# Spherical numbers of three chunks copied over rows by DMA, and both edge-weight layers in fp32 on two row halves

## What is computed

```python
wk = relu(edge_features @ k_w1 + k_b1) @ k_w2 + k_b2      # 64 -> 64 -> 128, and the same for wv
k  = wk * sum_s sh[e, s] * (x_dst @ Cqk[:, s, :])          # s = 0..8: nine spherical numbers of an edge
v  = wv * sum_s sh[e, s] * (x_dst @ Cv[:, s, :])
attn = sum over each head of q[edge_src] * k               # then a softmax over the edges of a node
upd  = sum over the edges of a node of v * alpha
```

## Time and profile before

| | |
|---|---|
| Median of 3 runs | 2944.04 us (2942.39 to 2945.2) |
| Profiled execution, its time | 2947.53 us |
| Its span in the trace | 2945.7 us |
| Busy share of the span: PE, DVE, ACT, POOL | 84%, 89%, 51%, 59% |
| Granted TensorE clock, mean | 0.899 of full speed; 1.00 within the loop |
| Stages: before the loop / loop / behind it | about 0 to 485 / 485 to 2771 / to 2946 us |
| DMA in all | 415 MB, 141 GB/s mean |

### The profile page before, as it was taken

One profiled execution on the slowest core, in us unless ns is written; L12 is line 12 of the kernel. 1 busy time (PEld: TensorE's weight loads), 2 busy tenths in 40 slices (PEclk: granted clock), 3 DMA queues, 4 the chain that ended last, 5 costly groups with the idle time before them and its releaser, 6 DMA issues.

```text
span 2945.7 us, 48186 instructions
## 1 busy us (share of the span) xinstructions
PE 2469.1 (84%) x12310; PEld 1787.3 (61%) x12505; DVE 2612.7 (89%) x3389; ACT 1514.6 (51%) x2914; POOL 1731.3 (59%) x1719
## 2 busy tenths in 40 slices
PE   2233347999999999999999999999999999999714
PEld 1233315677777776777677776777677777777511
DVE  6688835899999999999999999999999999999737
ACT  1321224566666655666566665666566566666310
POOL 1800037777777766667676666666666677665030
PEclk7555557999999999999999999999999999999855
DMA  6787714245555544444444444444445544544340
GB/s 187 202 222 187 210 25 111 76 131 149 148 149 145 148 147 139 141 142 148 139 144 142 146 147 140 140 144 147 142 141 147 148 141 142 148 144 132 121 124 11
DMA packets 282407, 415.35 MB, mean 141 GB/s; under 512 B 64463, under 2 KB 191875, under 8 KB 278470
## 3 DMA queue, kind: packets, MB, share of 16 engines
q1 hardware_dynamic: 222278, 296.67, 32.4%
q0 software_dynamic: 52704, 107.19, 15.1%
q10 hardware_dynamic: 7128, 8.13, 0.8%
...
## 4 chain that ended last, share of the span: by engine, by line
PE 52%; DVE 7%; issue 6%; ACT 3%; DMA 2%; POOL 2%; SPq 0%; DVEq 0%; ACTq 0%; POOLq 0%
PE bank L1118 11%; PE bank L1120 9%; PE bank L1119 9%; PE bank L1142 5%; PE bank L1163 4%; PE bank L1194 2%; PE bank L1124 2%; PE bank L1125 2%; PE bank L1095 2%; PE bank L1113 2%; DVE xa_t L1538 1%; DVE z_l L1546 1%; PE bank L1102 1%; POOL gathered L745 1%; PE bank L1101 1%
## 5 line engine op out<-in xcount | busy, mean ns | idle before, releaser
L745 POOL DMA_INDIRECT gathered<-xtab_d,src_g x784 | 780.6, 996 | 449.7 <-PE bank L1095 203.0
L745 POOL DMA_INDIRECT gathered<-qtab_d,dst_g x784 | 801.9, 1023 | 257.2 <-issue 249.0
L1118 PE MATMUL bank<-z_h,wt_h 128*128 128x512 f32 x1568 | 729.6, 465 | 27.9 <-DVE val L1578 27.9
L1538 DVE TENSOR_TENSOR xa_t<-bank,r_r 128x512 f32<-128x512 f32 x980 | 667.3, 683 | 13.5 <-PE bank L1142 10.3
L876 ACT ACTIVATE z_h<-xa_t 128x512 fp32r<-128x512 f32 x980 | 617.4, 634 | 110.1 <-DVE xa_t L1538 100.3
L1120 PE MATMUL bank<-z_h,wt_l 128*128 128x512 f32 x1568 | 620.7, 396 | 0.0
L1119 PE MATMUL bank<-z_l,wt_h 128*128 128x512 f32 x1568 | 618.8, 395 | 0.0
L1546 DVE TENSOR_TENSOR z_l<-xa_t,z_h 128x1024 fp32r<-128x1024 f32 x392 | 478.0, 1219 | 48.2 <-ACT z_h L876 44.6
L1118 PEld LDWEIGHTS bank<-z_h,wt_h 128*128 128x128 f32 x1568 | 301.1, 192 | 131.4 <-issue 92.7
L869 ACT ACTIVATE hid<-bank,b1kv 128x512 f32<-128x512 f32 x196 | 134.8, 688 | 476.4 <-PE bank L1102 462.4
L1120 PEld LDWEIGHTS bank<-z_h,wt_l 128*128 128x128 f32 x1568 | 294.9, 188 | 69.2
...
## 6 DMA issues: line engine op xcount, KB each, us to landing
nrow_d<-x_r SPq DMA_DIRECT2D x196, 288.0 KB
ea<-in_ea_t SPq DMA_DIRECT2D x392, 128.0 KB
exb<-exd_d SPq DMA_DIRECT2D x392, 128.0 KB
dmb<-exd_d SPq DMA_DIRECT2D x392, 128.0 KB
ea_c<-in_ea_t SPq DMA_DIRECT2D x49, 512.0 KB, 5.0
aggrow_d<-xa_t SPq DMA_DIRECT2D x49, 512.0 KB, 3.9
gathered<-xtab_d,src_g POOLq DMA_INDIRECT x784
gathered<-qtab_d,dst_g POOLq DMA_INDIRECT x784
```

The source lines that it names most:

```text
L745: rows_in = pool.indirect_dma_start(rows[:, c % 4, k, :], None, table, bass.IndirectOffsetOnAxis(ap=picked[:, s, at:at + 1], axis=0))
L1118: pe.matmul(ps[:, :], wt_h[rows, w, :], high, start=start, stop=False)
L1538: dve.tensor_tensor(z[:, i, :], bank[2 + (NJ * c + i) % 2][:, :], xt[:, c % 2, :], ALU.mult).then_inc(z_ok, 1)
```

## The change

- Chunks 0 and 1 (`NS = 2`) are spread by the TensorE as before, each now with a bank of its own. For chunks 2 to 4, SP's new `load_harmonics` issues six DMAs for each group, two groups ahead: each reads one row of 512 fp32 numbers from DRAM and writes it to 64 partitions of `sh_b` (two buffers).
- `outer` for chunks 2 to 4 is one multiplication of 128 x 1536 elements with both inputs in SBUF, in place of three of 128 x 512 with one input in PSUM. `outer_high` for them is one copy of 1536 elements in place of three.
- Both weight layers are done in fp32, without splits. `ea2` holds edges 0 to 255 on partitions 0 to 63 and edges 256 to 511 on 64 to 127, and the two loads of it are half as large. `hidden` is two fp32 matmuls of 256 columns, one on each row half, into banks 2 and 3 (the spread banks, free by then); it moves from before the products to behind `weights` and is done a body earlier. `weights` is four fp32 matmuls of 256 columns, for k on rows 0 to 63 and for v on rows 64 to 127 in turn.
- `edge_high`, `edge_low`, `hidden_low` and one of the two steps of `front_h` go; `front_h` is two steps of 256 columns in place of two of 512. The orders of the lists of ACT and DVE change as shown; `key_query` comes behind `sum_values`.
- Waits go with this: the spreads of group c wait for `hid_ok` of that group (ACT has read the banks), `hidden` waits for the two multiplications that read them, `load_edge` waits for `hid_ps` in place of `eal_ok`.
- The weights of the two layers leave the split table (`NW` 12 to 10), `exb` moves into a free part of `x_r`, and addresses in the loads are formed by round and place within it (`columns`).

The diff, cut to its core:

```diff
-CK, CV, W2KV, W1KV = 0, NJ, 2 * NJ, 2 * NJ + 1
-NW = 2 * NJ + 2
+CK, CV, CEND = 0, NJ, 2 * NJ
+NW = CEND
+NS = 2
+NZ = 3
...
-        ea2 = sb("ea2", [P, 2, G])
-        ea_hl = sb("ea_hl", [P, 2, G], F32R)
-        exb = sb("exb", [P, 2, G])
+        ea2 = sb("ea2", [P, 2, HG])
+        sh_b = sb("sh_b", [P, 2, NJ - NS, G])
...
             def load_edge(j, c):
-                past(sp, eal_ok, j, c, 2)
+                past(sp, hid_ps, j, c, 2, 2)
                 hold()
                 for half in range(2):
-                    sp.dma_start(ea2[half * D:(half + 1) * D, c % 2, :], edges_t[:, bass.ds(group(j, c) * G, G)]
-                                 ).then_inc(ea_in[c % 2], 16)
-                past(sp, shb_ps, j, c, 4, NJ)
+                    sp.dma_start(ea2[half * D:(half + 1) * D, c % 2, :],
+                                 columns(edges_t, j, c)[:, half * HG:(half + 1) * HG]).then_inc(ea_in[c % 2], 16)
+                past(sp, shb_ps, j, c, 4, NS)
                 hold()
                 if not isinstance(j, int) or c >= 2:
                     landed(sp, s3_in, j, c - 2)
                 hold()
-                sp.dma_start(s3[0:SP3, c % 4, :], sh3_d.rearrange("a s e -> (a s) e")[:, bass.ds(group(j, c) * G, G)]
-                             ).then_inc(s3_in[c % 2], 16)
+                sp.dma_start(s3[0:SP3, c % 4, :], columns(sh3_d.rearrange("a s e -> (a s) e"), j, c)).then_inc(s3_in[c % 2], 16)
+
+            def load_harmonics(j, c):
+                past(sp, z_ok, j, c, 2, NZ)
+                hold()
+                for i in range(NS, NJ):
+                    for half in range(2):
+                        k = min(2 * i + half, S - 1)
+                        sp.dma_start(sh_b[half * D:(half + 1) * D, c % 2, i - NS, :],
+                                     columns(harmonics_t[k:k + 1, :], j, c).to_broadcast([D, G])
+                                     ).then_inc(sh_b_in[c % 2], 16)
...
             def body(j, c):
+                if live(j, c + 2):
+                    load_harmonics(j, c + 2)
                 if live(j, c + 3):
...
-            def edge_high(j, c):
-                landed(act, ea_in, j, c, 32)
-                past(act, hid_ps, j, c, 2)
-                act.activation(ea_hl[:, c % 2, :], ea2[:, c % 2, :], ACT.Copy).then_inc(eah_ok, 1)
             def front_h(j, c):
-                done(act, hid_ps, j, c)
+                done(act, hid_ps, j, c, 2)
+                past(act, wk_ps, j, c, 1)
                 past(act, wv_ps, j, c, 1)
-                act.activation(hid[:, :], ps_hw[:, :], ACT.Relu, bias=b1kv[:, :]).then_inc(hid_ok, 1)
-                act.activation(hid_h[:, :], ps_hw[:, :], ACT.Relu, bias=b1kv[:, :]).then_inc(hid_ok, 1)
+                for f in range(2):
+                    act.activation(hid[:, f * HG:(f + 1) * HG], bank[2 + f][:, 0:HG], ACT.Relu, bias=b1kv[:, :]
+                                   ).then_inc(hid_ok, 1)
 
             def outer_high(j, c, i):
                 if i == 0:
                     past(act, acc_ps, j, c, 2)
-                done(act, z_ok, j, c, NJ, i + 1 - NJ)
-                act.activation(z_h[:, c % 2, i, :], z[:, i, :], ACT.Copy).then_inc(zh_ok, 1)
+                done(act, z_ok, j, c, NZ, i + 1 - NZ)
+                chunks = slice(i, i + 1) if i < NS else slice(NS, NJ)
+                act.activation(z_h[:, c % 2, chunks, :], z[:, chunks, :], ACT.Copy).then_inc(zh_ok, 1)
 
             def front_q(j, c):
                 done(act, qt_ps, j, c)
...
@@ -918,8 +939,6 @@
                                .rearrange("p f h w -> p (f h) w"), ACT.Copy).then_inc(row_ok, 1)
 
             def body(j, c):
-                if live(j, c + 1):
-                    front_h(j, c + 1)
                 s = batch_at(c, 8)
                 if live_batch(j, s):
                     batch_scores(j, s)
@@ -937,13 +956,11 @@
                 if live_batch(j, s):
                     batch_turned(j, s)
                 if live(j, c + 1):
+                    outer_high(j, c + 1, 2)
+                if live(j, c + 2):
+                    front_h(j, c + 2)
+                if live(j, c + 1):
                     weights_v(j, c + 1)
-                    outer_high(j, c + 1, 2)
-                    outer_high(j, c + 1, 3)
-                if live(j, c + 2):
-                    edge_high(j, c + 2)
-                if live(j, c + 1):
-                    outer_high(j, c + 1, 4)
                 if live(j, c - LAG):
                     rows(j, c - LAG)
...
                 tr.then_inc(xt_ps, 1)
 
             def hidden(j, c):
-                done(pe, eal_ok, j, c)
-                past(pe, wv_ok, j, c, 1)
-                pe.matmul(ps_hw[:, :], wt_h[:, W1KV, :], ea_hl[:, c % 2, :], start=True, stop=False)
-                pe.matmul(ps_hw[:, :], wt_l[:, W1KV, :], ea_hl[:, c % 2, :], start=False, stop=True
-                          ).then_inc(hid_ps, 1)
+                landed(pe, ea_in, j, c, 32)
+                if not isinstance(j, int) or c >= 1:
+                    done(pe, z_ok, j, c - 1, NZ, NS - NZ)
+                for f in range(2):
+                    half = slice(f * D, (f + 1) * D)
+                    pe.matmul(bank[2 + f][:, 0:HG], w1kv[half, :], ea2[half, c % 2, :], start=True, stop=True
+                              ).then_inc(hid_ps, 1)
 
             def q_turn(j, c):
                 landed(pe, qg_in, j, c, 64)
...
@@ -1125,22 +1144,25 @@
                 return pe.matmul(ps[:, :], wt_l[:, w, :], both, start=False, stop=True)
 
             def weights(j, c):
-                done(pe, hidl_ok, j, c)
+                done(pe, hid_ok, j, c, 2)
+                past(pe, wv_ok, j, c, 1)
                 if isinstance(j, int) and c + 1 >= NG:
                     pe.wait_ge(xt_ok, NG)
                 else:
                     done(pe, xt_ok, j, c + 1)
-                for ps, rows, done_ps in ((ps_xw, slice(0, D), wk_ps), (ps_hw, slice(D, P), wv_ps)):
-                    split_matmul(ps, W2KV, hid_h[rows, :], hid_l[rows, :], True, True, rows).then_inc(done_ps, 1)
+                for f in range(2):
+                    edges = slice(f * HG, (f + 1) * HG)
+                    mk = pe.matmul(ps_xw[:, edges], w2kv[0:D, :], hid[0:D, edges], start=True, stop=True)
+                    mv = pe.matmul(ps_hw[:, edges], w2kv[D:P, :], hid[D:P, edges], start=True, stop=True)
+                mk.then_inc(wk_ps, 1)
+                mv.then_inc(wv_ps, 1)
 
             def spread(j, c, i):
 
                 if i == 0:
                     landed(pe, s3_in, j, c)
-                if not isinstance(j, int) or c * NJ + i >= 2:
-                    done(pe, z_ok, j, c, NJ, i - 1 - NJ)
-                pe.matmul(bank[2 + (NJ * c + i) % 2][:, :], sel[:, i, :], s3[:, c % 4, :], start=True, stop=True
-                          ).then_inc(shb_ps, 1)
+                    done(pe, hid_ok, j, c, 2)
+                pe.matmul(bank[2 + i][:, :], sel[:, i, :], s3[:, c % 4, :], start=True, stop=True).then_inc(shb_ps, 1)
 
             def products(j, c, i):
                 done(pe, zl_ok, j, c, NLOW, i // 2 + 1 - NLOW)
...
@@ -1197,22 +1219,21 @@
 
             def body(j, c):
                 if live(j, c + 1):
-                    spread(j, c + 1, 0)
-                    spread(j, c + 1, 1)
+                    for i in range(NS):
+                        spread(j, c + 1, i)
                 if live(j, c + 2):
                     x_turn(j, c + 2)
                 if live(j, c - 2):
                     scores(j, c - 2)
                 if live(j, c + 1):
-                    hidden(j, c + 1)
                     q_turn(j, c + 1)
                 for i in range(NJ):
                     if live(j, c):
                         products(j, c, i)
-                    if i + 2 < NJ and live(j, c + 1):
-                        spread(j, c + 1, i + 2)
                     if i == 1 and live(j, c + 1):
                         weights(j, c + 1)
+                    if i == 1 and live(j, c + 2):
+                        hidden(j, c + 2)
                     s = batch_at(c, 10)
                     if i == 1 and live_batch(j, s):
                         batch_turn(j, s, c)
...
@@ -1531,16 +1552,22 @@
 
             def outer(j, c, i):
 
-                done(dve, shb_ps, j, c, NJ, i + 1 - NJ)
                 if i == 0:
                     done(dve, xt_ok, j, c)
                     past(dve, acc_ps, j, c, 2)
-                dve.tensor_tensor(z[:, i, :], bank[2 + (NJ * c + i) % 2][:, :], xt[:, c % 2, :], ALU.mult
-                                  ).then_inc(z_ok, 1)
+                    past(dve, zl_ok, j, c, 1, NLOW)
+                if i < NS:
+                    done(dve, shb_ps, j, c, NS, i + 1 - NS)
+                    dve.tensor_tensor(z[:, i, :], bank[2 + i][:, :], xt[:, c % 2, :], ALU.mult).then_inc(z_ok, 1)
+                else:
+                    landed(dve, sh_b_in, j, c, 32 * (NJ - NS))
```

(29 more changed lines are left out.)

39 lines of the change are left out of this document (24 added, 15 removed).

## The result

The changed kernel is **slower**: 3105.62 us (median of 4 runs, 3083.97 to 3113.12) against 2944.62 (4 runs, 2942.39 to 2946.51), a ratio of 1.0535 with a 95% interval of 1.0477 to 1.0593. Forecast were 2842 us and a range up to 2990. The profiled execution took 3112.78 us, its span is 3111.0.

What follows compares the result with a forecast made beforehand. PE was taken as the bound: 11.68 - 0.49 - 0.14 = 11.05 us a group, plus 0.1 for POOL close by, 11.15. Saving 0.53 over 195 groups, 103 us, took 2947.5 to 2844, median 2842 us; range 2795 to 2990.

Steps and rivals of the forecast that it cites:

- What bounds before: Loop of the kernel before: PE is the bound; POOL allows at most 0.77 us a group to be gained.
- PE's term: Matmuls of a group: three spreads and the old layers go, six fp32 matmuls come; -0.49 us a group.
- fully paired: Six fp32 matmuls on PE: both row halves work side by side, 1.49 us, PE -0.60 a group.
- in-between case: Six fp32 matmuls on PE: one of twelve halves stays alone at an end, 1.71 us, PE -0.38 a group.
- rival of unpaired fp32: fp32 matmuls on PE's row halves run one behind the other: PE +0.69 a group, 3051 us; chance 0.12.
- DVE's term: VectorE: three products and two steps go, a 1536-element product of 1.75 us comes; about 9.9 us a group.
- SP's term: SP's queue issuing the loads: six added loads and a wait cost 4.0, giving 10.5 us a group.
- SP becomes the bound: SP's load queue sets the pace from 0.82 us per load on: 2989 to about 3145 us; chance 0.12.
- POOL's term: POOL's gathers: stretching goes from 0.68 to about 0.75 us a group, POOL to 11.0.
- POOL binds: Stretching of POOL's gathers up to double: 11.4 to 11.6 us a group, 2889 to 2928 us; chance 0.11.
- The forecast's own case: Whole kernel: PE 11.05, POOL 11.0, about 11.15 us a group, 2795 to 2885 us; chance 0.60.
- The lower case: Whole loop better than forecast: all matmuls paired and POOL unstretched, 10.9 us a group, 2795 us.

Runs made afterwards that it cites:

- e7: The changed kernel with three gathers per table in place of four, a quarter of the edges getting their neighbours' rows: 2816.73 us.
- e10: e8 with the six loads issued for the first two groups only, later groups multiplying by those numbers: 2810.75 us.
- e8: e5 with the 512-column scan of `sum_values` done as two scans of 256, nothing left out: 2838.63 us.
- e2: The changed kernel with the six loads issued for the first two groups only, the product unchanged: 3095.53 us.
- e4: The kernel before with the six loads of each group added into a tile that nothing reads: 2948.47 us.
- e3: The changed kernel with the 1536-element product split into three of 512 on the same tiles: 2926.88 us.
- e9: The kernel before with each 1024-element subtraction cut into two of 512 and the scan into two of 256: 2954.33 us.
- e5: e3 with each subtraction of 1024 elements (`outer_low`) done as two of 512, nothing left out: 2846.33 us.
- e6: The changed kernel with its 1536-element product kept that long but reading a PSUM bank in place of `sh_b`: 2945.73 us (one run).

## Why the prediction was wrong

**What bounds before: right.** PE was the bound, with POOL 0.8 to 0.9 us a group behind it.

**PE's term: right in kind, 0.11 us too dear.** It had -0.49 us, between -0.60 (fully paired) and +0.69 (not paired). PE's timeline of the changed kernel at the six fp32 matmuls (start, length, line):

```profile
2007.24 0.48 PE L1155 MATMUL bank<-hid,w2kv 64*128 64x256 f32 x1
2007.24 0.48 PE L1156 MATMUL bank<-hid,w2kv 64*128 64x256 f32 x1
2007.56 0.38 PE L1155 MATMUL bank<-hid,w2kv 64*128 64x256 f32 x1
2007.57 0.38 PE L1156 MATMUL bank<-hid,w2kv 64*128 64x256 f32 x1
...
2008.21 0.60 PE L1121 MATMUL bank<-ea,w1kv 64*128 64x256 f32 x4
2008.73 0.50 PE L1137 MATMUL bank<-z_h,wt_h 128*128 128x512 f32 x1
```

From 2007.24 to 2008.73 are 1.49 us, exactly the fully paired price; each half (two instructions in fp32) starts with its partner. The in-between case of 1.71 didn't occur, so of the rule of the Trainium skill (TensorE: Matmul & The Clock Gate, "The mechanism" of Part 3) the overlap of row groups is seen, and the lag that I had drawn from its program order is not. With -0.60 PE's own need would be 10.94. No run shows that as a group: e7 has 11.09, where SP is at its limit, and e10 has 11.01, where POOL is. The rival of unpaired fp32 falls.

**DVE's term: right.** The product was put at 1.75 us and takes 1750 ns.

**SP's term: too small, and hidden in the change.** It had 10.5 us a group, "under 11, by half a microsecond". In e7 and e8 SP works 11.1: 6.8 instead of 6.45 without the loads, and 4.3 for the six instead of 4.0. In the changed kernel it still waits for DVE (`x_r`, line 1630: 326.7 us in 133 times from 500 to 2900 us), so it isn't the bound there. The rival "SP becomes the bound" asked for 0.82 us a load and a time above before; a load costs 0.7. So SP makes nothing slower than before, but it stands above PE, and with POOL relieved it, not PE, sets the pace: e10 puts that at 28 us. The DMA share is 0.67 of 12.68, 8.5 us a group against 7.7 to 8.2, and hidden (e2, e4).

**POOL's term: wrong, and it decided.** The step that failed is "in proportion, stretching goes from 0.68 to about 0.75, POOL to 11.0; if it doubled, POOL would need 11.6". Stretching is 8 x 0.284 = 2.27 us a group, over three times the base, and POOL needs 12.5. It went wrong twice.

- *The measure.* I scaled with the total time of DVE instructions with two SBUF inputs (6.4 to 6.8 us, up by 6%). What counts is what is left of one when a gather starts, and that goes with the square of the length: 2.45 to 3.46 us² in a body, up by 41%. e3 shows it, with a total that is longer and a loss that is gone. The row that I had cited for it carries the law already: a gather of 1.38 us under an instruction that ended 0.56 after its start.
- *The base.* 0.68 us (0.085 a gather) is well under half of what random starts would have given in the kernel before (0.21). Its gathers fell mostly outside the instructions that hold them, or near their ends: from 1500 to 1700 us 46 of 138 started under one with more than 0.12 us of it left, but only 16 took more than 1.1 us. After the change 59 of 126 did so, and 52 took more than 1.1. The price read from the old order of the loop didn't carry over to the new one. By size this is the larger part: from 0.07 to 0.21 it is the starts, from 0.21 to 0.27 the lengths. This division is worked out, not measured by a run of its own.

The rival "POOL binds" named the mechanism and had 0.11; its price stopped at a doubling, 11.6 us a group, and so it ended below before. Had its upper end been taken from random starts, 8 x (0.944 + 0.27 + 0.305) + 0.25 = 12.4, it would have been the rival on the slower side: 2947.5 + (12.4 - 11.7) x 195 = about 3084. The forecast's own case asked for POOL to hold at 11.0 with PE at 11.05, a margin of nothing, on the one term that rested on an analogy. The lower case needed short instructions: e8, at 2838.63, is where the forecast of 2842 had been. That it lands there is luck. The forecast had PE at 11.05 as the bound and 0.1 for two engines at the same limit; in e8 SP has 11.1 and POOL 11.07, and PE needs 11.01 at most (e10). (By its own terms the sum gives 2844 less 3.5, 2840.5 and not 2842; nothing hangs on it.)

**Open.** Why the starts in before, e4 and e9 (0.06 to 0.07) fall so well, and those of e3, e5, e8 and e10 better than at random, isn't settled. That POOL takes its pace from PE in the first three, and so keeps a fixed place in the body, is argued only; so is that in the others gathers fall in step with short instructions, as the rows of e8 show it for a stretch. That SP bounds e7 and e8 is read from its waits; no run takes the loads out of e7. The spread of the changed kernel's runs, 3084 to 3113 us, has no cause shown either. Nor did a run separate the fp32 layers from the spreads that the loads replace: how much of e8's gain each brings isn't known.

## What to carry to other kernels

Before an operand moves from PSUM to SBUF on VectorE, or small instructions are joined into a long one, look at what GpSimd does meanwhile: if its indirect gathers are within some 10% of the bound (7% here), price them with random starts (the square of each length), not with the stretching that the present order happens to show. That price is a mean and no upper end: in the change, e6 and e7 the measured stretching is 0.01 us above it. Where the gathers do bind, cut VectorE's instructions with two SBUF inputs: two of the three cuts cost about 9 us in the kernel before, where they weren't needed; all three brought 267 where they were (3106 to 2839). And when an engine is relieved, price the third engine, and the queue behind it, as carefully as the first: here POOL made the change slower, and with POOL relieved SP took its place.
